# Score weights spread from one line by four products on one row group, and fewer, wider warm-up products, in a top-k cross-attention kernel

## The chip, the cores and the metric

The kernel runs on one core of a Trainium2 chip. The metric is the device time of one execution in microseconds; the time before is the median of three runs.

## What is computed

The reference, cut to what matters (B = 8 batches, N = 224 rows of x, S = 750 context rows, D = 512, 16 heads of 32, TOPK = 10):

```python
scores = jnp.einsum('bnd,d->bn', base_hidden, score_w[0]) + score_b[0]
_, topk_idx = jax.lax.top_k(scores, TOPK)
sparse_hidden = jnp.take_along_axis(base_hidden, topk_idx[:, :, None], axis=1)
q = (sparse_hidden @ Wq.T + bq)   # split into heads; k and v from scaffold_hidden (the context)
logits = jnp.einsum('bhqd,bhkd->bhqk', q, k) * scale
attn = jax.nn.softmax(logits, axis=-1)
o = jnp.einsum('bhqk,bhkd->bhqd', attn, v)
attn_out = o @ out_w.T + out_b
return base_hidden.at[jnp.arange(B)[:, None], topk_idx].set(attn_out)
```

All of it is float32.

## The kernel before

Each engine has its own hand-written program, and semaphores order them. The batches are taken in two groups: batches 0 and 1 first, then 2 to 7, so that attention on the first two can start while the other rows are still being scored.

The start runs as follows. SyncE's queue issues, in this order, x of batches 0 and 1, wq, x of 2, wk, x of 3 and 4, the context columns of batch 0 in two halves, x of 5 to 7, the columns of batch 1, and the context rows of 0 and 1. ScalarE's queue issues the score row (L265, into `score_quarters`, four partitions 0, 32, 64, 96, each with a quarter of the weights and the bias) and the biases (L266).

TensorE's program (L762 on) is: two warm-up products (`keep_warm(WARM_WEIGHTS)`, L561), `spread_score_w` (L567), which copies the score weights to 112 partitions by multiplying each quarter with a column of ones, ten warm-up products, `transpose_scores(0)` (L575), ten warm-up products, `spread_idx` (L581), `pick_rows` (L590, takes the chosen rows out of x by one-hot products), one warm-up product, `join_rows` (L600), `project_queries(0)` (L632), `fold_keys` (L645, folds the queries into the key weights, so keys are never formed), `dot_key_bias(0)` (L677), and the logits of batch 0 in the order in which the folded queries come (L700). A warm-up product multiplies a matrix of ones by 128 columns into a part of PSUM that nobody reads. TensorE executes its queue in order, so what stands behind a warm-up product waits for it.

VectorE copies the spread weights from PSUM (`copy_score_w`, L341, and the bias, L342) after one wait for all four products, forms the scores of a batch by two multiply-and-add passes over 112 partitions (L350), adds the bias (L363), and after the transposes finds the top ten with their positions (L366 to L376) and writes `idx_diag` (L378), for which L581 waits. After it come one-hot masks (L386), and ScalarE and VectorE copy the picked parts (L270, L393).

From then on TensorE alternates between logits (L700, L714) and mixing the context rows with the softmax weights (L731), with loads of context columns and rows issued as buffers come free; VectorE computes the shift of the softmax (L444 to L482) and ScalarE the exponential (L306). At the end the values are projected (L746), then the output (L758), and the rows are scattered into the output (L259).

Every float32 product at these lines stands in the trace as two weight loads (PEld) and two products (PE), each of one pass over the columns.

Of the kernel before, what the change touches and what calls it, by code (L numbers as in the profile page):

```python
# [21 lines left out]
B, N, D, S = 8, 224, 512, 750  # L22
HEADS, TOPK = 16, 10
DH = D // HEADS
P = 128
DT = D // P
# [4 lines left out]
X_P = N // 2  # L31
# [8 lines left out]
QUAD = 32  # L40
CB = HQ // QUAD
QUADS = P // QUAD
QK_UNITS = 2 * QK_STEPS
WARM_WEIGHTS, WARM_SCORES, WARM_CHOICE, WARM_N = 2, 10, 10, 128
FIRST = GROUPS[0][1]
PART = 32
TILE = 64
# [3 lines left out]
def build(nc, x, x_lines, ctx_rows, ctx_cols, wq, wk, wv, wo, in_bias, out_b, score_row, out):  # L51
# [5 lines left out]
    with stack:  # L57
        def sb(name, shape, dt=F32):
            return stack.enter_context(nc.sbuf_tensor(name, shape, dt))

        def ps(name, shape):
            return stack.enter_context(nc.psum_tensor(name, shape, F32))

        def sem(name):
            return stack.enter_context(nc.semaphore(name))
# [7 lines left out]
        bias_sb = sb("bias_sb", [P, 3, DT])  # L73
        out_b_sb = sb("out_b_sb", [BQ, D])
        score_w_sb = sb("score_w_sb", [X_P, D])
        score_quarters = sb("score_quarters", [P, P + 1])
        score_b_sb = sb("score_b_sb", [X_P, 1])
        ctx_c = [sb(f"ctx_c{n}", [P, DT, S_T, S_P]) for n in range(2)]
        ctx_r = [sb(f"ctx_r{n}", [P, S_T, D]) for n in range(2)]
# [1 line left out]
        ones = sb("ones", [P, P])  # L81
# [42 lines left out]
        logits_ps = [ps(f"logits_ps{n}", [P, 2, 512]) for n in range(2)]  # L124
# [6 lines left out]
        score_w_ps = mix_ps + misc_ps  # L131
# [9 lines left out]
        score_w_in, bias_in, out_b_in = sem("score_w_in"), sem("bias_in"), sem("out_b_in")  # L141
# [6 lines left out]
        score_w_ps_done, score_w_done = sem("score_w_ps_done"), sem("score_w_done")  # L148
# [113 lines left out]

        @block.scalar
        def _(act):
            act.dma_start(score_quarters[0:P:QUAD, :], score_row).then_inc(score_w_in, 16)  # L265
            act.dma_start(bias_sb[:, :, :], in_bias).then_inc(bias_in, 16)  # L266

            def copy_parts():
                act.wait_ge(parts_ps_done, 1)
                nc.scalar.activation(parts[:, 0:D // 2], parts_ps[0], ACT.Copy).then_inc(parts_done, 1)  # L270

            def copy_queries(g):
                b0, b1 = GROUPS[g]
                act.wait_ge(picked_T_ps, g + 1)
                nc.scalar.activation(picked_T[g][:, :, :], picked_ps[g][:, 0:DT * b1 * TOPK]  # L275
                                     .rearrange("p (t q) -> p t q", t=DT), ACT.Copy).then_inc(picked_T_done, 1)

            def copy_pairs():
                b0, b1 = GROUPS[1]
                for step in range(QK_STEPS):  # L280
                    act.wait_ge(pair_done, step + 1)
                    nc.scalar.activation(
                        qk[:, b0:b1, step, :].rearrange("p b (e r c) -> p r e b c", e=DT, r=2)[:, 0],
                        pair_ps[step % 2][0][:, 0:HQ // 2 * (b1 - b0)].rearrange("p (e b c) -> p e b c", e=DT, b=b1 - b0),
                        ACT.Copy).then_inc(low_copied, 1)

            def copy_fold():
                for step in range(QK_STEPS):
                    act.wait_ge(qk_ps, step + 1)
                    nc.scalar.activation(qk[:, 0:FIRST, step, :].rearrange("p b (e c) -> p e b c", e=DT),  # L290
                                         fold_ps[step][:, 0:HQ * FIRST].rearrange("p (e b c) -> p e b c", e=DT, b=FIRST),
                                         ACT.Copy).then_inc(qk_done, 1)

            def copy_key_rows():
                act.wait_ge(key_dot_ps, 1)
                for e in range(DT):
                    nc.scalar.activation(
                        key_rows[:, 0:FIRST, e, :],
                        key_ps[0][e * QUAD:(e + 1) * QUAD, 0:HC * FIRST].rearrange("p (b c) -> p b c", b=FIRST),
                        ACT.Copy).then_inc(key_rows_done, 1)  # L300

            def exponential(b, n):
                for k in range(2):
                    act.wait_ge(shifted, 2 * b + k + 1)
                    part = probs[n][:, k * BANK_T:(k + 1) * BANK_T, :]
                    nc.scalar.activation(part, part, ACT.Exp, scale=SCALE).then_inc(exp_done, 1)  # L306

            def copy_mix(b, half):
                act.wait_ge(mix_ready[half], b + 1)
                nc.scalar.activation(mix[:, 2 * half:2 * half + 2, :, b * TOPK:(b + 1) * TOPK],  # L310
                                     mix_ps[half][:, 0:2 * HQ].rearrange("p (t h q) -> p t h q", t=2, h=HEADS),
                                     ACT.Copy).then_inc(mix_out[half], 1)

            copy_parts()
            copy_queries(0)
            copy_fold()
            copy_key_rows()
            act.dma_start(out_b_sb[:, :], out_b.broadcast_to([BQ, D])).then_inc(out_b_in, 16)
            exponential(0, 0)
            copy_mix(0, 0)  # L320
            exponential(1, 1)
            copy_mix(0, 1)
            copy_mix(1, 0)
            copy_queries(1)
            copy_mix(1, 1)
            copy_pairs()
            exponential(2, 0)
            for b in range(3, B):
                copy_mix(b - 1, 0)
                exponential(b, b % 2)  # L330
                copy_mix(b - 1, 1)
            copy_mix(B - 1, 0)
            copy_mix(B - 1, 1)
# [2 lines left out]
        @block.vector  # L336
        def _(dve):
            def copy_score_w():
                dve.wait_ge(score_w_ps_done, 1)
                for r in range(QUADS):  # L340
                    nc.vector.tensor_copy(score_w_sb[:, r * P:(r + 1) * P], score_w_ps[r][0:X_P, 0:P]).then_inc(score_w_done, 1)  # L341
                nc.vector.tensor_copy(score_b_sb[:, :], score_w_ps[0][0:X_P, P:P + 1]).then_inc(score_w_done, 1)  # L342
                dve.wait_ge(score_w_done, QUADS + 1)

            def score(b, rows=(0, 1)):
                dve.wait_ge(x_in[b], 16)
# [164 lines left out]
            nc.vector.tensor_copy(row_name[:, :, :], row_name_i[:, :, :]).then_inc(vec_consts, 1)  # L511
            dve.wait_ge(vec_consts, 4)
            copy_score_w()
            score(0)
            score(1)
# [40 lines left out]

        @block.tensor
        def _(pe):
            def keep_warm(n):
                for _ in range(n):  # L560
                    nc.tensor.matmul(logits_ps[1][:, 1, 0:WARM_N], ones[:, :], ones[:, 0:1].broadcast_to([P, WARM_N]),  # L561
                                     start=True, stop=True)

            def spread_score_w():
                pe.wait_ge(score_w_in, 16)
                for r in range(QUADS):
                    last = nc.tensor.matmul(score_w_ps[r][0:X_P, 0:P + 1], ones[r * QUAD:r * QUAD + 1, 0:X_P],  # L567
                                            score_quarters[r * QUAD:r * QUAD + 1, :], start=True, stop=True)
                last.then_inc(score_w_ps_done, 1)

            def transpose_scores(g):
                b0, b1 = GROUPS[g]
# [11 lines left out]
            def pick_rows():  # L584
                pe.wait_ge(hot_done, 1)
                for half in range(2):
                    for b in range(FIRST):
                        for j in range(2):
                            at = (2 * b + j) * PART
                            last = nc.tensor.matmul(parts_ps[half][at:at + PART, :], one_hot[:, b, j, :],  # L590
                                                    x_sb[0:X_P, b, j, half * (D // 2):(half + 1) * (D // 2)],
                                                    start=True, stop=True)
                    last.then_inc(parts_ps_done, 1)

            def join_rows():
                pe.wait_ge(regroup_done, 2 * FIRST + 1)
                pe.wait_ge(parts_done, 2)
                for t in range(DT):
                    for j in range(P // TILE):
                        last = nc.tensor.matmul(picked_ps[0][j * TILE:(j + 1) * TILE, t * FIRST * TOPK:(t + 1) * FIRST * TOPK],  # L600
                                                parts[:, t * P + j * TILE:t * P + (j + 1) * TILE],
                                                regroup[:, :, :].rearrange("p b q -> p (b q)"), start=True, stop=True)
                last.then_inc(picked_T_ps, 1)
# [157 lines left out]

            pe.wait_ge(vec_consts, 1)  # L762
            keep_warm(WARM_WEIGHTS)
            spread_score_w()
            keep_warm(WARM_SCORES)
# [2 lines left out]
            keep_warm(WARM_CHOICE)  # L768
            spread_idx()
            pick_rows()  # L770
            keep_warm(1)
            join_rows()
            pe.wait_ge(wq_in, 16)
            project_queries(0)
# [58 lines left out]
```

## Time and profile before

| | |
|---|---|
| median of 3 runs | 148.5 us (148.49, 148.50, 149.54) |
| the profiled execution | 149.29 us, span 147.1 us |
| instructions in the span | 3011 |
| TensorE products (PE) | 136.9 us busy, 93%, 1292 records |
| TensorE weight loads (PEld) | 130.6 us busy, 89%, 1292 records |
| VectorE | 81.2 us busy, 55% |
| ScalarE | 23.2 us busy, 16% |
| GpSimd | 4.8 us busy, 3% |
| HBM traffic | 254 GB/s over the span |

The span is the time from the first to the last instruction of the profiled execution; 2.2 us of its time lie around it. Times in all rows are microseconds from the start of the span unless marked ns. PE stands for TensorE's products, PEld for its weight loads, DVE for VectorE, ACT for ScalarE, POOL for GpSimd, SP for SyncE; L and a number is the line of the kernel.

### The profile page before, as it was taken

Reading aid. Unit: us, or ns where it says so; the run is one execution under the profiler, and the core shown is the slowest. Engines: PE = TensorE matmul, PEld = TensorE weight load, DVE = VectorE, ACT = ScalarE, POOL = GpSimd, SP = SyncE. Lnnn points to the kernel's source line nnn. Section 1 sums busy time; section 2 is a strip of 40 time slices with the busy share of each in tenths; the row PEclk is TensorE's granted clock in tenths of the full one; section 3 lists DMA queues with packets and bytes.
Section 4 is the critical chain, followed back from the end, with each engine's and each line's share of the span. In section 5 each row is a group of like instructions: output and inputs, shape, how many; then the busy total and the mean of one; then the engine's idle time right before and its main releaser. Section 6 shows DMA issues by size and latency. Waiting matters only on the chain.

```text
span 147.1 us, 3011 instructions
## 1 busy us (share of the span) xinstructions
PE 136.9 (93%) x1292; PEld 130.6 (89%) x1292; DVE 81.2 (55%) x214; ACT 23.2 (16%) x48; POOL 4.8 (3%) x24
## 2 busy tenths in 40 slices
PE   3899868999999999999999999999999999999980
PEld 2896858999999998999999999999999999998840
DVE  1666654897893347457974286057318705745330
ACT  3001032002042034003041014004101400411100
POOL 6000000002000000000000000000000000000002
PEclk9999999999999999999999999999999999999999
DMA  4999999999857439989998994998691181000001
GB/s 150 417 423 414 417 416 426 370 419 415 250 226 254 178 77 391 399 317 417 413 408 274 301 347 125 304 300 331 196 324 46 20 357 50 0 4 0 4 0 45
DMA packets 5733, 37.61 MB, mean 256 GB/s; under 512 B 805, under 2 KB 809, under 8 KB 3417
## 3 DMA queue, kind: packets, MB, share of 16 engines
q1 hardware_dynamic: 5344, 36.93, 66.6%
q0 software_dynamic: 128, 0.33, 0.7%
q8 instruction: 10, 0.16, 0.5%
q10 hardware_dynamic: 248, 0.17, 0.4%
q14 instruction: 3, 0.02, 0.0%
HBM read 33.60 MB, written 3.83 MB: 254 GB/s over the span
## 4 chain that ended last, share of the span: by engine, by line
PE 89%; DVE 3%; issue 2%; DMA 2%; ACT 1%; POOLq 1%; DVEq 0%
PE mix_ps L731 36%; PE logits_ps L714 22%; PE logits_ps L700 11%; PE logits_ps L561 5%; PE logits_ps L632 3%; PE logits_ps L758 2%; DMA score_quarters<-score_row_dram 2%; PE logits_ps L666 1%; PE mix_ps L666 1%; PE misc_ps L746 1%; PE mix_ps L645 1%; ACT probs L306 1%; POOLq L57 1%; PE logits_ps L590 1%; PE misc_ps L645 1%
## 5 line engine op out<-in xcount | busy, mean ns | idle before, releaser
L731 PE MATMUL mix_ps<-probs,ctx_r 125*128 125x160 f32 x384 | 54.0, 300 | 0.2 <-ACT probs L306 0.2
L731 PEld LDWEIGHTS mix_ps<-probs,ctx_r 125*128 125x128 f32 x384 | 52.6, 190 | 1.0 <-issue 0.9
L714 PE MATMUL logits_ps<-qk,ctx_c 128*125 128x160 f32 x240 | 33.4, 300 | 0.0
L714 PEld LDWEIGHTS logits_ps<-qk,ctx_c 128*125 128x125 f32 x240 | 32.9, 188 | 0.0
L444 DVE TENSOR_REDUCE col_max<-logits_ps 125x160 f32<-125x960 f32 x8 | 9.2, 1154 | 25.7 <-PE logits_ps L714 21.3
L700 PE MATMUL logits_ps<-qk,ctx_c 128*125 128x160 f32 x144 | 20.5, 302 | 0.0
L700 PEld LDWEIGHTS logits_ps<-qk,ctx_c 128*125 128x125 f32 x144 | 19.6, 188 | 0.5 <-issue 0.4
L310 ACT ACTIVATE mix<-mix_ps 128x320 f32<-128x320 f32 x16 | 7.0, 439 | 64.5 <-PE mix_ps L731 64.5
L482 DVE TENSOR_REDUCE prob_sum<-probs 125x160 f32<-125x960 f32 x8 | 14.6, 1837 | 4.0 <-ACT probs L306 4.0
L306 ACT ACTIVATE probs<-probs 125x480 f32<-125x480 f32 x16 | 9.3, 603 | 28.1 <-DVE probs L476 28.1
L561 PE MATMUL logits_ps<-ones 128*128 128x128 f32 x46 | 9.3, 378 | 1.1 <-DVE ones L507 1.1
L350 DVE CUSTOM_DVE_ANT_0 product<-x_sb,score_w_sb 112x512 f32<-112x512 f32 x16 | 10.1, 681 | 0.0
L561 PEld LDWEIGHTS logits_ps<-ones 128*128 128x128 f32 x46 | 8.6, 284 | 1.8 <-DVE ones L507 1.1
L476 DVE TENSOR_TENSOR probs<-logits_ps,shift 125x480 f32<-125x480 f32 x16 | 9.8, 653 | 0.3
L632 PE MATMUL logits_ps<-picked_T,wq_sb 128*64 128x20 f32 (+1 forms) x128 | 4.1, 218 | 0.4 <-ACT picked_T L275 0.4
L632 PEld LDWEIGHTS logits_ps<-picked_T,wq_sb 128*64 128x64 f32 x128 | 3.9, 138 | 0.7 <-issue 0.7
L259 POOL DMA_INDIRECT out_dram<-y_sb,row_idx x1 | 0.9, 922 | 110.1 <-DVE y_sb L504 110.1
L466 DVE COPY head_shift<-head_shift 32x5 f32<-32x5 f32 x24 | 3.9, 163 | 0.8
L405 DVE TENSOR_TENSOR q_sb<-logits_ps,bias_sb 128x40 f32<-128x40 f32 (+1 forms) x4 | 1.0, 242 | 6.1 <-PE logits_ps L632 6.1
L454 DVE COPY quad_max<-quad_max 32x5 f32<-32x5 f32 x24 | 3.8, 160 | 0.8
L487 DVE RECIPROCAL inv_sum<-misc_ps 128x320 f32<-128x320 f32 x1 | 2.2, 2157 | 3.5 <-PE misc_ps L684 3.5
L758 PE MATMUL logits_ps<-wo_sb,o_T 128*80 128x256 f32 x16 | 3.7, 382 | 0.0
(97 smaller groups left out, 74.0 us busy)
## 6 DMA issues: line engine op xcount, KB each, us to landing
ctx_r<-ctx_rows_dram SPq DMA_DIRECT2D x8, 1536.0 KB, 7.7
ctx_c<-ctx_cols_dram SPq DMA_DIRECT2D x6, 1500.0 KB, 8.4
x_sb<-x_lines_dram SPq DMA_DIRECT2D x8, 512.0 KB, 10.6
out_dram<-x_sb SPq DMA_DIRECT2D x8, 448.0 KB, 12.6
ctx_c<-ctx_cols_dram SPq DMA_DIRECT2D x4, 750.0 KB, 15.8
wq_sb<-wq_dram SPq DMA_DIRECT2D x1, 1024.0 KB, 6.7
wk_sb<-wk_dram SPq DMA_DIRECT2D x1, 1024.0 KB, 9.7
wv_sb<-wv_dram SPq DMA_DIRECT2D x1, 1024.0 KB, 8.6
```

The costliest lines, as they stand in the source:

```text
L306: nc.scalar.activation(part, part, ACT.Exp, scale=SCALE).then_inc(exp_done, 1)
L310: nc.scalar.activation(mix[:, 2 * half:2 * half + 2, :, b * TOPK:(b + 1) * TOPK], mix_ps[half][:, 0:2 * HQ].rearrange("p (t h q) -> p t h ...
L350: nc.vector.tensor_tensor_reduce(out=products[j][:, :], in0=x_sb[0:X_P, b, j, :], in1=score_w_sb[:, :], scale=1.0, scalar=0.0, op0=ALU.mul ...
L444: nc.vector.tensor_reduce(col_max[0:S_P, :], tiles(n).rearrange("p k t c -> p c k t"), AX.XY, ALU.max)\
L476: nc.vector.tensor_tensor(probs[n][:, k * BANK_T:(k + 1) * BANK_T, :], tiles(n)[:, k, :, :], shift[0:S_P, :].unsqueeze(1).broadcast_to([S_ ...
L482: nc.vector.tensor_reduce(prob_sum[:, b, :], probs[n][:, :, :].rearrange("p t c -> p c t"), AX.X, ALU.add)\
L561: nc.tensor.matmul(logits_ps[1][:, 1, 0:WARM_N], ones[:, :], ones[:, 0:1].broadcast_to([P, WARM_N]), start=True, stop=True)
L632: last = nc.tensor.matmul(query_ps[g][half][j * TILE:(j + 1) * TILE, k * nq:(k + 1) * nq], wq_sb[:, t, c:c + TILE], picked_T[g][:, t, b0 * ...
L700: last = nc.tensor.matmul(logits_ps[n][0:S_P, t // BANK_T, (t % BANK_T) * HQ:(t % BANK_T + 1) * HQ], ctx_c[n][:, f, t, :], qk[:, b, f, :], ...
L714: last = nc.tensor.matmul(logits_ps[n][0:S_P, t // BANK_T, (t % BANK_T) * HQ:(t % BANK_T + 1) * HQ], ctx_c[n][:, f, t, :], qk[:, b, f, :], ...
L731: last = nc.tensor.matmul(mix_ps[half][:, f * HQ:(f + 1) * HQ], ctx_r[n][0:S_P, t, c:c + P], probs[n][:, t, :], start=(t == 0), stop=(t == ...
L758: last = nc.tensor.matmul(logits_ps[0][0:BQ, half, 0:D // 2], o_T[:, e, :], wo_sb[:, e, cols], start=(e == 0), stop=(e == DT - 1))
```

## The change

The score weights lie in one line of one partition (`score_line`, 512 weights and the bias). The four products that spread them all read partition 0, each signals its own end, and VectorE copies each as it comes; the bias is the last column of the fourth. The number of the products is still four (QUADS and DT are both 4). The warm-up products get widths of their own: one of 256 columns in place of two of 128 ahead of the weights, 512, 256 and 128 in place of ten of 128 ahead of the transposes, 512, 256 and 256 in place of ten of 128 ahead of the index spread, and one of 128 as before ahead of the join.

```diff
-WARM_WEIGHTS, WARM_SCORES, WARM_CHOICE, WARM_N = 2, 10, 10, 128
+WARM_WEIGHTS, WARM_SCORES, WARM_CHOICE, WARM_PARTS = (256,), (512, 256, 128), (512, 256, 256), (128,)
-        score_quarters = sb("score_quarters", [P, P + 1])
+        score_line = sb("score_line", [1, D + 1])
-            act.dma_start(score_quarters[0:P:QUAD, :], score_row).then_inc(score_w_in, 16)
+            act.dma_start(score_line[:, :], score_row).then_inc(score_w_in, 16)
             def copy_score_w():
-                dve.wait_ge(score_w_ps_done, 1)
-                for r in range(QUADS):
+                for r in range(DT):
+                    dve.wait_ge(score_w_ps_done, r + 1)
                     nc.vector.tensor_copy(score_w_sb[:, r * P:(r + 1) * P], score_w_ps[r][0:X_P, 0:P]).then_inc(score_w_done, 1)
-                nc.vector.tensor_copy(score_b_sb[:, :], score_w_ps[0][0:X_P, P:P + 1]).then_inc(score_w_done, 1)
-                dve.wait_ge(score_w_done, QUADS + 1)
+                nc.vector.tensor_copy(score_b_sb[:, :], score_w_ps[DT - 1][0:X_P, P:P + 1]).then_inc(score_w_done, 1)
+                dve.wait_ge(score_w_done, DT + 1)
-            def keep_warm(n):
-                for _ in range(n):
-                    nc.tensor.matmul(logits_ps[1][:, 1, 0:WARM_N], ones[:, :], ones[:, 0:1].broadcast_to([P, WARM_N]),
+            def keep_warm(widths):
+                for n in widths:
+                    nc.tensor.matmul(logits_ps[1][:, 1, 0:n], ones[:, :], ones[:, 0:1].broadcast_to([P, n]),
                                      start=True, stop=True)
             def spread_score_w():
                 pe.wait_ge(score_w_in, 16)
-                for r in range(QUADS):
-                    last = nc.tensor.matmul(score_w_ps[r][0:X_P, 0:P + 1], ones[r * QUAD:r * QUAD + 1, 0:X_P],
-                                            score_quarters[r * QUAD:r * QUAD + 1, :], start=True, stop=True)
-                last.then_inc(score_w_ps_done, 1)
+                for r in range(DT):
+                    c = P + (r == DT - 1)
+                    nc.tensor.matmul(score_w_ps[r][0:X_P, 0:c], ones[0:1, 0:X_P], score_line[:, r * P:r * P + c],
+                                     start=True, stop=True).then_inc(score_w_ps_done, 1)
-            keep_warm(1)
+            keep_warm(WARM_PARTS)
```

On the host, `score_row` becomes one row of 513 numbers in place of four of 129.

## Rows read from the trace of the kernel before

**Rows 1.** The page: busy us, share and instructions of each engine; the instruction queue.
```profile
PE 136.9 (93%) x1292; PEld 130.6 (89%) x1292; DVE 81.2 (55%) x214; ACT 23.2 (16%) x48; POOL 4.8 (3%) x24
...
q8 instruction: 10, 0.16, 0.5%
```

**Rows 2.** The chain in order of time, 16 to 28 us: start, us, what.
```profile
16.01 2.05 PE logits_ps L632 x64
...
20.63 1.91 issue
...
22.88 5.63 PE logits_ps L700 x40
```

**Rows 3.** The timeline, 4 to 13 us: start, us, engine and line, idle before.
```profile
4.13 0.56 PE L567 MATMUL mix_ps<-score_quarters,ones 1*112 1x129 f32 x2 [1.84 <-DMA score_quarters<-score_row_dram]
4.14 0.56 PE L567 MATMUL misc_ps<-score_quarters,ones 1*112 1x129 f32 x2
...
4.48 0.42 PE L567 MATMUL mix_ps<-score_quarters,ones 1*112 1x129 f32 x2
...
5.06 0.49 DVE L341 COPY score_w_sb<-mix_ps 112x128 f32<-112x128 f32 x2 [2.70 <-PE misc_ps L567]
...
5.86 0.15 DVE L342 COPY score_b_sb<-mix_ps 112x1 f32<-112x1 f32 x1
6.05 0.69 DVE L350 CUSTOM_DVE_ANT_0 product<-x_sb,score_w_sb 112x512 f32<-112x512 f32 x1
...
8.62 0.23 DVE L363 TENSOR_SCALAR biased_scores<-scores,score_b_sb 112x4 f32<-112x4 f32 x1
...
9.28 0.58 PE L575 MATMUL misc_ps<-ident,biased_scores 112*2 112x112 f32 x2
...
12.07 0.23 DVE L378 SCALAR_TENSOR_TENSOR idx_diag<-top_idx,row_base,own_batch 2x20 f32<-2x20 uint32 x1
...
12.58 0.37 PE L581 MATMUL misc_ps<-idx_diag,ones 2*112 2x20 f32 x2
```

**Rows 4.** Timeline of TensorE from 5.5 and from 11.1; L561's durations in both.
```profile
5.22 4.05 PE L561 MATMUL logits_ps<-ones 128*128 128x128 f32 x18
...
10.93 1.73 PE L561 MATMUL logits_ps<-ones 128*128 128x128 f32 x14
...
L561 PE MATMUL logits_ps<-ones 128*128 128x128 f32 x17 | 4.0, 431 | 0.0
...
L561 PE MATMUL logits_ps<-ones 128*128 128x128 f32 x12 | 1.5, 273 | 0.0
```

**Rows 5.** Who waited for whom, TensorE's products: us in total, times, longest.
```profile
PE logits_ps L677 <- issue: 1.9, 1, 1.9
...
PE mix_ps L731 <- ACT probs L306: 0.2, 1, 0.2
```

**Rows 6.** DMA queue of instructions in windows 20:21, 26.6:28, 40.6:42: packets, MB, share.
```profile
q8 instruction: 1, 0.02, 6.9%
...
q8 instruction: 1, 0.02, 4.9%
...
q8 instruction: 1, 0.02, 4.0%
```

**Rows 7.** Windows: length, TensorE busy (records), clock, DMA share, GB/s.
```profile
0.00:16.00 16.00, 12.18 (x90) 1.00 0.90 358
...
0.00:20.70 20.70, 16.80 (x221) 1.00 0.93 369
...
0.00:40.70 40.70, 34.77 (x354) 1.00 0.95 375
...
136.81:139.16 2.35, 2.35 (x129) 1.00 0.04 7
```

**Rows 8.** DMA issues in 5.4:6.95 and 6.95:9.7 us: count, KB each, median us to landing.
```profile
x_sb<-x_lines_dram SPq DMA_DIRECT2D x3, 512.0 KB, 15.2
...
ctx_c<-ctx_cols_dram SPq DMA_DIRECT2D x2, 750.0 KB, 18.7
```

More of the change, by code:

```diff
@@ L820 @@
         "out_b": np.asarray(L0_xattn_out_b).reshape(1, D),
-        "score_row": np.concatenate([np.asarray(L0_xattn_score_w).reshape(QUADS, P),
-                                     np.tile(np.asarray(L0_xattn_score_b).reshape(1, 1), (QUADS, 1))], axis=1),
+        "score_row": np.concatenate([np.asarray(L0_xattn_score_w).reshape(1, D),
+                                     np.asarray(L0_xattn_score_b).reshape(1, 1)], axis=1),
     }
```

## The prediction

> **What bounds the kernel.** I read the page first: TensorE's products are busy 93% of the span [rows 1], so time is won where TensorE is held up or does what nobody needs. The chain of work that ended last, in order of time, tells where that is. Up to 23 us it runs over the landing of the score row, warm-up products (L561), two small products for the choice of rows (L575, L581), the query and key products, and 1.91 us called "issue" [rows 2]. From 22.9 us on it is logits and mixing products back to back. All that the change touches lies before 16 us. A microsecond won there is won at the end, if nothing later absorbs it: the longest wait of TensorE's products after the 1.9 us one is 0.2 us [rows 5], and the transfers, which could absorb it, are looked at below.
>
> The timeline of 4 to 13 us [rows 3] shows who holds whom. L567's eight records run in two rounds of four, 4.13 to 4.92, since the four products lie on four different row groups. VectorE copies from 5.06 and scores from 6.05. The sum with the bias (L363) ends at 8.85, but L575 starts at 9.28, because ten warm-up products stand before it in TensorE's queue. idx_diag (L378) ends at 12.30, but L581 starts at 12.58, again behind ten. So in this execution warm-up holds the path by 0.39 and 0.25 us.
>
> The clock of TensorE doubles inside the second ten. The granted-clock column says 1.00 throughout, but the spacing tells it [rows 4]: 18 records from 5.22 span 4.05 us, which is (4.05 - 0.43) / 17 = 0.213 us from start to start; 14 from 10.93 span 1.73 us, (1.73 - 0.27) / 13 = 0.112. That is 1.66 and 0.875 ns per column, the levels 1.2 and 2.4 GHz at two cycles a column. Until then TensorE had been working without a gap since 4.13.
>
> **Part 1, the score weights.** One row of 2 KB in one partition is sent in place of four of 0.5 KB; the transfer is mostly latency (L567 waits for it until 4.13, rows 3), and I take its landing as unchanged, within 0.3 us either way. The four products now use the same row group, so eight records follow each other. From rows 3 and 4: the second starts 0.35 after the first (4.13, 4.48), the rest 0.213 apart, the last at 4.13 + 0.35 + 6 x 0.213 = 5.76, and it ends 0.42 later, 6.18. The copies run behind the products, which hides three of them: the fourth starts 0.14 after its product (as 5.06 after 4.92), 6.32. Then come one copy's spacing, 0.20 (four in 5.06 to 5.86), and the bias copy's, 0.19. The first score starts at 6.71 instead of 6.05: **+0.66 us**. The three added waits are covered by the products. The bounds: +0.5 if the products pack a little closer, +0.95 with the late landing. Rows 3 show what is given up: products on different row groups start 0.01 us apart (4.13, 4.14). The Trainium skill, "TensorE: Matmul & The Clock Gate", Part 3 (row/col tiling), speaks against this part: small products whose operands start at partitions 0, 32, 64 and 96 run at once, those on one row group do not; by its figure of 3.07 times for four packed products the eight records would take about 2.4 us instead of 0.79, an estimate, and the score would start at 7.0; by the rows it is 6.71.
>
> **Part 2, the warm-up products.** L575's data is now ready at 8.85 + 0.66 = 9.51. The warm-up ahead of it is 512 + 256 + 128 = 896 columns, two records each: 2 x 896 x 1.66 ns = 2.98 us. It starts at about 6.1 with 0.16 for its first gap (4.85 to 5.22), and ends its issue near 9.25. It no longer holds L575, which starts at 9.54, 0.26 later than before instead of 0.66 later. idx_diag then ends at 12.30 + 0.26 = 12.56. The second warm-up is 1024 columns, 2048 with both records. If the clock doubles at 10.93 as before, 1.02 us from 9.91 do 613 of them and the other 1435 take 1.26 us: done at 12.19, under VectorE's chain. L581 starts at 12.60 instead of 12.58. So of the 0.66 us, 0.02 to 0.1 is left in this execution; I take **+0.05**. keep_warm between picking and joining is one product of 128 columns as before.
>
> In an execution whose clock doubles before 8.5 us the old kernel loses nothing to warm-up: 0.39 + 0.25, and L575's second record follows 0.1 sooner and is shorter, together about 0.8 us (estimate from rows 3 and 4). The profiled execution took 149.29 us (span 147.1 and 2.2 around it), and the three runs 148.49, 148.50 and 149.54. The difference of 0.8 to the two fast ones is just that size. I take them for such executions; there the whole **+0.66** is paid.
>
> **Part 3, the instruction stream.** Each product at this line is two weight loads and two products. Fifteen fewer calls (23 before, 8 after) are 60 instructions less. This matters for the 1.91 us. L677 waits for nothing between its eight records, yet three run and five come 1.91 us later [rows 2, 5]. In that gap the only odd transfer is one packet of the instruction queue between 20 and 21 us [rows 6]. The page has ten such packets for 2 x 1292 TensorE instructions, 258 for each (rows 1 and 6), so one per 129 records. The stall comes at record 221. Counting back 129, TensorE passed record 92 at 16.07 us (90 by 16.0, rows 7). A packet near 40.7 us comes at record 354 [rows 6, 7], 133 after the stall, and TensorE waits for nothing there. So passing one block boundary asks for the block after the next boundary. From 16.07 to the restart at 22.55 is 6.5 us; the next boundary is passed at 22.55 and its packet comes after 26.6 [rows 6], again four microseconds in the crowd of loads. The block between took only 4.6 us to execute, because L632 runs a record each 0.032 us [rows 2] and L645 is of the same kind. That is why just this one is late.
>
> With 30 records fewer ahead, the first boundary falls at old record 122, 16.01 + 32 x 0.032 = 17.03, and the block is there at 23.5. The second falls at old record 251: with the stall gone L700 starts at 20.97, and 25 of its records later, at 5.63 / 40 = 0.141 each, it is 24.5. Cover 1.0 us; **the stall goes, -1.91**.
>
> **What would absorb it.** Everything from L700 on starts 1.9 us earlier. The context columns of batch 1 are issued from 6.99 and land 18.7 later in the median, near 26 [rows 8], where the second logits, now at 27.8, take them in halves; those of batch 0 stand ahead of the last x loads in the queue and land before them. The last three x loads are issued from 5.46 and take 15.2 in the median [rows 8], so they land from about 20 to 23; VectorE, held by the same stall today, would want them at 22.5, 23.7 and 25.0 (two records of 0.69 each, rows 3, at 0.61 spacing). All later loads are issued on TensorE's progress and move with it. Nothing takes the 1.9 back.
>
> **Sum.** Profiled execution: 149.29 - 1.91 + 0.05 = 147.4. Against the median: 148.5 - 1.91 + 0.66 = 147.25. The runs shown are what will be compared, so I forecast **147.2 us**, and 146.6 if the median execution is one where the 0.66 is covered.
>
> **Rivals.**
> - *The wait for code moves and does not vanish* (15%). The stall falls into L700 if the block takes over a microsecond longer than 6.5. For it: one sample, in a full DMA queue. Against it: cover 1.0 us. At its full price: 148.5 + 0.66 = 149.2; half of it, 148.2.
> - *The idle is not code* (5%). If the first 442 instructions and the next lie in TensorE's memory from the start, the 1.91 us has another cause, tied to the key products themselves, and stays: 148.5 + 0.66 = 149.2. The packet at 20 us, and ten packets in all, speak against it. The Trainium skill, "Runtime: NRT & Kernel Launch", Instruction fetch mechanics, is on this rival's side: it gives TensorE room for 2048 instructions and calls the refills mostly hidden.
> - *The clock stays at 1.2 GHz* (10%), the slower one. TensorE now idles from 9.25 to 9.54 and does 1.7 us of one-row products at 4.13, where it had worked on without a gap before its clock rose. It decides at 12.6: if the clock is low there, the second warm-up ends at 9.91 + 2048 x 1.66 ns = 13.3, L581 waits 0.7, L590 (16 records of 256 columns, four at a time) costs 4 x 256 x 0.79 ns = 0.8 more, and L632's 2.05 us [rows 2] up to 2.05 more, of which I take 1.8: 147.25 + 3.3 = 150.6.
> - *A wait for code at the end* (5%). A boundary falls late in L746 (129 records in 2.35 us, rows 7) and its block is asked for some 4 us earlier. The queues are idle then; up to 1 us: 148.2.
> - Mine: 65%, 146.6 to 147.9.
>
> **Range and chances.** 146.3 (row landing early, warm-up cover) to 149.4 (stall stays). A measurement of this kernel tells about 1% from no change, so faster means below 147.0. My case is split by that line: faster 0.33, within 1% 0.56 (with the rivals at 148 to 149.6), slower 0.11.
>
> **What would show it.** Right: L567 one after another, first score near 6.7, L575 waiting for L363, no issue wait at L677, L700 starting near 21 instead of 22.8 and L731 as much earlier, and the later steps unchanged. Wrong: an issue wait inside L700 or L746; L561 still 0.21 us per 128 columns after 11 us and L590 or L632 longer; or a landing of score_line well after 4.1.

## The result

The changed kernel takes 146.4 us (median of 4 runs, 146.26 to 146.50) against 148.61 for the kernel before (4 runs, 148.49 to 149.54). The ratio is 0.984, 95% interval 0.980 to 0.987: faster by 1.6%. Forecast were 147.2 us and 0.9%, with more chance for "within 1%" than for "faster"; the time lies inside the range, near its lower end, and the gain is nearly twice the one forecast. Two later sets of six runs gave ratios of 0.989 (0.982 to 0.995) and 0.988 (0.983 to 0.993). All sixteen executions of the changed kernel have a median of 146.44 us, with thirteen from 145.97 to 147.32 and three from 148.1 to 149.0. The second set alone has a median of 147.04. Executions of one kernel differ by up to some microseconds here, so medians are given with their extremes. The profiled execution took 146.49 us, its span 144.3, 2.8 less than before.

The timeline of the profiled changed kernel (start, us, engine and line, what it writes and reads, idle before):

```profile
0.74 0.51 ACTq L265 DMA_DIRECT2D score_line<-score_row_dram  x1
...
2.22 1.19 PE L568 MATMUL mix_ps<-score_line,ones 1*112 1x128 f32 x4
...
3.21 1.06 PE L568 MATMUL misc_ps<-score_line,ones 1*112 1x128 f32 x4
...
4.51 0.15 DVE L342 COPY score_b_sb<-misc_ps 112x1 f32<-112x1 f32 x1
4.69 0.69 DVE L350 CUSTOM_DVE_ANT_0 product<-x_sb,score_w_sb 112x512 f32<-112x512 f32 x1
...
7.29 0.23 DVE L363 TENSOR_SCALAR biased_scores<-scores,score_b_sb 112x4 f32<-112x4 f32 x1
...
7.67 0.53 PE L575 MATMUL misc_ps<-ident,biased_scores 112*2 112x112 f32 x2
...
10.69 0.37 PE L581 MATMUL misc_ps<-idx_diag,ones 2*112 2x20 f32 x2 [0.18 <-DVE idx_diag L378]
...
18.42 0.35 PE L677 MATMUL logits_ps<-q_diag,key_rep 128*32 128x80 f32 x8
18.69 5.70 PE L700 MATMUL logits_ps<-qk,ctx_c 128*125 128x160 f32 x40
```

Three things are to be seen beside [rows 2, 3]. The products that spread the weights start at 2.22 us instead of 4.13. They run one after another and the first score starts 2.47 us behind them instead of 1.92. And L677 runs all its eight records without a pause, so that L700 starts at 18.69. The queues show what became early. In the kernel before, whose timeline this is, the same load took twice as long to issue, beside the first two x loads:

```profile
0.75 0.85 SPq L186 DMA_DIRECT2D x_sb<-x_lines_dram  x2
0.75 1.09 ACTq L265 DMA_DIRECT2D score_quarters<-score_row_dram  x1
```

The DMA queues' packets say where the time went: those of ScalarE's queue (q10) beside those of SyncE's (q1), first from 1.6 to 1.8 us in the changed kernel, then from 3.3 to 4.1 us in the kernel before, which has none of q10 between 1.6 and 3.3 (packets, MB, share of 16 engines; half of the q10 packets shown carry the row, the other half its signals):

```profile
q1 hardware_dynamic: 5, 0.02, 35.3%
q10 hardware_dynamic: 2, 0.00, 3.4%
```

```profile
q10 hardware_dynamic: 8, 0.00, 1.2%
```

In both kernels the first packets of x start at 1.77 us. The packet of the row starts at 1.65 in the changed kernel, ahead of them, and takes 0.1 us. In the kernel before, where the issue ended at 1.84, the four packets start at 3.53 and take 0.03 us each: the row was waiting, not moving.

By L700 the changed kernel is 4.1 us ahead. It arrives with 2.8. This is where the rest went, in the timeline of the changed kernel, 23.9 to 26.5 us:

```profile
24.00 0.69 DVE L350 CUSTOM_DVE_ANT_0 product<-x_sb,score_w_sb 112x512 f32<-112x512 f32 x1 [0.51 <-DMA x_sb<-x_lines_dram]
...
25.35 0.23 DVE L363 TENSOR_SCALAR biased_scores<-scores,score_b_sb 112x12 f32<-112x12 f32 x1
...
25.64 0.35 PE L575 MATMUL misc_ps<-ident,biased_scores 112*6 112x112 f32 x2 [1.24 <-DVE biased_scores L363]
```

The last x load lands at 24.0 us (at 23.1 in the kernel before, where VectorE came to it at 26.8). VectorE waits for it, scores it, and TensorE, which has put the transposes of the second group into the middle of the logits of batch 0, waits 1.24 us for VectorE (1.55 and 0.56 us in the other two profiles of this kernel, where it landed at 24.3 and 23.5). The chain of the changed kernel now runs over that transfer, which none of the edits makes earlier:

```profile
6.39 17.59 DMA x_sb<-x_lines_dram
```

A table of the two profiled executions, start of each step in us:

| step | before | after | ahead |
|---|---|---|---|
| spread of the weights | 4.13 | 2.22 | 1.91 |
| first score (L350) | 6.05 | 4.69 | 1.36 |
| L581 | 12.58 | 10.69 | 1.89 |
| L632 | 16.01 | 14.13 | 1.88 |
| L700 of batch 0 | 22.81 | 18.69 | 4.12 |
| L731 of batch 0 | 37.14 | 34.35 | 2.79 |
| end of span | 147.1 | 144.3 | 2.8 |

### The profile page after: what moved, and what is told of

Its sections match the earlier page's. It is cut to its first block, busy times and chain, and to the rows that moved or that the text cites. A ratio compares the mean times of both kernels' runs of the same rounds, so it can differ in the third digit from the quotient of the medians.

```text
span 144.3 us, 2951 instructions
## 1 busy us (share of the span) xinstructions
PE 136.3 (94%) x1262; PEld 127.3 (88%) x1262; DVE 81.8 (57%) x214; ACT 23.1 (16%) x48; POOL 4.7 (3%) x24
## 4 chain that ended last, share of the span: by engine, by line
PE 76%; DMA 12%; SPq 4%; DVE 3%; issue 1%; POOLq 1%; ACT 1%; DVEq 0%
PE mix_ps L731 37%; PE logits_ps L714 23%; DMA x_sb<-x_lines_dram 12%; PE logits_ps L700 7%; PE logits_ps L758 3%; SPq L186 2%; PE logits_ps L666 2%; PE logits_ps L632 1%; PE mix_ps L666 1%; DVE product L350 1%; PE misc_ps L746 1%; ACT probs L306 1%; POOLq L57 1%; PE logits_ps L746 1%; SPq L179 1%
## 5 line engine op out<-in xcount | busy, mean ns | idle before, releaser
L731 PE MATMUL mix_ps<-probs,ctx_r 125*128 125x160 f32 x384 | 54.0, 300 | 0.2 <-ACT probs L306 0.2
L731 PEld LDWEIGHTS mix_ps<-probs,ctx_r 125*128 125x128 f32 x384 | 52.5, 190 | 1.0 <-issue 0.9
L700 PE MATMUL logits_ps<-qk,ctx_c 128*125 128x160 f32 x144 | 20.5, 301 | 0.0
L700 PEld LDWEIGHTS logits_ps<-qk,ctx_c 128*125 128x125 f32 x144 | 19.6, 188 | 0.5 <-issue 0.4
L482 DVE TENSOR_REDUCE prob_sum<-probs 125x160 f32<-125x960 f32 x8 | 14.6, 1836 | 4.0 <-ACT probs L306 4.0
L350 DVE CUSTOM_DVE_ANT_0 product<-x_sb,score_w_sb 112x512 f32<-112x512 f32 x16 | 10.4, 688 | 1.1 <-DMA x_sb<-x_lines_dram 1.1
L561 PE MATMUL logits_ps<-ones 128*128 128x256 f32 (+2 forms) x16 | 7.6, 615 | 1.1 <-DVE ones L507 1.1
L561 PEld LDWEIGHTS logits_ps<-ones 128*128 128x128 f32 x16 | 4.1, 284 | 3.8 <-issue 2.5
L632 PE MATMUL logits_ps<-picked_T,wq_sb 128*64 128x20 f32 (+1 forms) x128 | 4.1, 218 | 0.4 <-ACT picked_T L275 0.4
L632 PEld LDWEIGHTS logits_ps<-picked_T,wq_sb 128*64 128x64 f32 x128 | 3.9, 138 | 0.7 <-issue 0.7
## 6 DMA issues: line engine op xcount, KB each, us to landing
x_sb<-x_lines_dram SPq DMA_DIRECT2D x8, 512.0 KB, 10.9
```

What stands on the lines that cost most here:

```text
L350: nc.vector.tensor_tensor_reduce(out=products[j][:, :], in0=x_sb[0:X_P, b, j, :], in1=score_w_sb[:, :], scale=1.0, scalar=0.0, op0=ALU.mul ...
L482: nc.vector.tensor_reduce(prob_sum[:, b, :], probs[n][:, :, :].rearrange("p t c -> p c t"), AX.X, ALU.add)\
L561: nc.tensor.matmul(logits_ps[1][:, 1, 0:n], ones[:, :], ones[:, 0:1].broadcast_to([P, n]), start=True, stop=True)
L632: last = nc.tensor.matmul(query_ps[g][half][j * TILE:(j + 1) * TILE, k * nq:(k + 1) * nq], wq_sb[:, t, c:c + TILE], picked_T[g][:, t, b0 * ...
L700: last = nc.tensor.matmul(logits_ps[n][0:S_P, t // BANK_T, (t % BANK_T) * HQ:(t % BANK_T + 1) * HQ], ctx_c[n][:, f, t, :], qk[:, b, f, :], ...
L731: last = nc.tensor.matmul(mix_ps[half][:, f * HQ:(f + 1) * HQ], ctx_r[n][0:S_P, t, c:c + P], probs[n][:, t, :], start=(t == 0), stop=(t == ...
```

## The experiments

TensorE's granted clock differs between executions here: in four profiles (`e1_line`, `e2_warm`, `e4_bias_first`, `e9_wide`) it falls to half in a stretch that lies between 14.6 and 23.3 us. The mean granted clock of the whole execution, which stands on record for every execution, is 0.969 to 0.977 in those four. It does not show a late first rise: before the rise that column reads 1.00 as well, as in the kernel before, whose L561 ran at 1.66 ns a column until 10.9 us.

**The early row: two ways to make it late again.** In `e4_bias_first` ScalarE's two loads change places; in `e5_four_pieces` the row goes into the one partition in four pieces of 516 bytes (the products' reads and the row on the host follow, not shown).

```diff
 e4_bias_first, against the changed kernel
-            act.dma_start(score_line[:, :], score_row).then_inc(score_w_in, 16)
             act.dma_start(bias_sb[:, :, :], in_bias).then_inc(bias_in, 16)
+            act.dma_start(score_line[:, :], score_row).then_inc(score_w_in, 16)
```

```diff
 e5_four_pieces, against the changed kernel
-        score_line = sb("score_line", [1, D + 1])
+        score_line = sb("score_line", [1, QUADS, P + 1])
-            act.dma_start(score_line[:, :], score_row).then_inc(score_w_in, 16)
+            act.dma_start(score_line[:, :, :], score_row[:, :, 0:P + 1]).then_inc(score_w_in, 16)
```

> The changed kernel with ScalarE's two loads exchanged: the biases (128 partitions) are issued first, the score line second, so that the line is issued behind the first x loads. Theory A (the row came early since its one packet was put in ahead of the x packets): L568 starts at 3.5 to 4.5 instead of 2.2; of that delay about 1.2 us is covered by the wait for the last x load; median 147.0 to 147.6. Rival D (it came early since it is one packet in one partition, wherever it stands): L568 starts before 3.2; median under 146.7.

> The changed kernel with the score row sent into one partition in four pieces of 516 bytes (gaps between them in DRAM) instead of one of 2052. Theory A1 (the four pieces are what made the issue of the load take 1.09 us and put it behind the x packets): the issue takes about 1.1 us again and L568 starts near 4.1; fastest executions 147.2 to 147.8. Theory A2 (four partitions, spread over several DMA engines, are what did it): issue 0.5 us, L568 at 2.2 to 2.5, fastest executions near 146.4.

Timeline of `e4_bias_first`, then of `e5_four_pieces`:

```profile
1.18 0.54 ACTq L266 DMA_DIRECT2D score_line<-score_row_dram  x1
...
4.71 0.55 PE L568 MATMUL mix_ps<-score_line,ones 1*112 1x128 f32 x1 [2.42 <-DMA score_line<-score_row_dram]
```

```profile
0.76 1.19 ACTq L265 DMA_DIRECT2D score_line<-score_row_dram  x1
...
4.10 1.19 PE L568 MATMUL mix_ps<-score_line,ones 1*112 1x128 f32 x4 [1.81 <-DMA score_line<-score_row_dram]
```

The line issued in 0.54 us, but 0.4 us later, is used 2.5 us later: 148.0 us (147.74 to 150.63, 11 executions, ratio 0.996, interval 0.993 to 0.999). The line in four pieces takes 1.19 us to issue and is used when the quarters were: 147.23 us (146.99 to 148.58, 10 executions, ratio 0.992, interval 0.989 to 0.996). The packets fit both. In `e5` those of the row start at 3.36 to 3.49, behind the first of x (1.75); in `e4` the one packet starts at 3.96, behind those of x and behind all 128 packets of the biases in its own queue. So the row is early where its one piece is issued before the first x packets go (1.75 to 1.77 in all these runs); that it lies in one partition is not enough. Whether `e4` is late for its 0.4 us or for standing behind the biases is not separated. Rival D is out. `e4` came out above its range (147.0 to 147.6): L568 started at 4.71, later than the 3.5 to 4.5 that I had put. In `e5` Theory A1 holds, with its fastest executions at 146.99, a little under the range. `e5` is the changed kernel with the landing that the prediction assumed, and it takes what the prediction said: 147.2. Part of that agreement is luck, since the terms are off one by one, as shown below.

**The wait at L677: the count of instructions alone.** `e3_count` cuts the same columns into more products, `e9_wide` merges those of the kernel before.

```diff
 e3_count, against the changed kernel (60 instructions more)
-WARM_WEIGHTS, WARM_SCORES, WARM_CHOICE, WARM_PARTS = (256,), (512, 256, 128), (512, 256, 256), (128,)
+WARM_WEIGHTS, WARM_SCORES, WARM_CHOICE, WARM_PARTS = (128,) * 2, (128,) * 7, (64,) * 11 + (160,) * 2, (128,)
```

```diff
 e9_wide, against the kernel before (60 instructions fewer)
-WARM_WEIGHTS, WARM_SCORES, WARM_CHOICE, WARM_N = 2, 10, 10, 128
+WARM_WEIGHTS, WARM_SCORES, WARM_CHOICE, WARM_PARTS = (256,), (512, 512, 256), (512, 512, 256), (128,)
```

> The changed kernel with the same warm-up columns (256, 896, 1024, 128) cut into 2, 7, 13 and 1 products instead of 1, 3, 3 and 1: 60 instructions more, nothing else. Theory A: the issue wait is back inside L677, 1.3 to 2 us; up to 1.2 us of it is covered by the wait for the last x load, which falls in L575's wait; median 0.3 to 0.8 above the changed kernel's 146.4. Rival B: no issue wait, the same time within 0.2.

> The kernel before with its warm-up columns unchanged (256, 1280, 1280, 128) but in 1, 3, 3 and 1 products instead of 2, 10, 10 and 1; quarters and four row groups as before. Only the count of TensorE's instructions falls, by 60. Theory A: no issue wait at L677, L575 and L581 start as before (9.3 and 12.6 or earlier), the clock behaves as in the kernel before; fastest executions 146.0 to 146.6, median 146.6 to 147.2. Rival B (the wait belongs to the key products): the wait stays, median 148.2 to 148.6.

TensorE's timeline in `e3_count` near L677:

```profile
18.97 0.33 PE L677 MATMUL logits_ps<-q_diag,key_rep 128*32 128x80 f32 x3
20.67 0.34 PE L677 MATMUL logits_ps<-q_diag,key_rep 128*32 128x80 f32 x5 [1.38 <-issue]
```

The wait is back, after the same third record of eight, although L677 runs 1.3 us earlier than in the kernel before. Of all that the change took out, only the 60 instructions were put back; the row is as early and the columns are as few as in the changed kernel. It is 1.38 us here, inside what was expected. The time is not: 148.72 us (147.41 to 152.15, 10 executions, ratio 0.998, interval 0.993 to 1.003) against an expected 146.7 to 147.2. Two things besides the wait are in it. A pass of 64 columns takes 0.112 us at the higher clock, as much as one of 128, so the second warm-up takes 3.3 us instead of 2.5 and L581 starts 0.55 later in the profile (147.41 us). And three of the ten executions are above 150; two of these have a mean granted clock of 1.000, and none was profiled, so their cause is open. `e1_line` below has the same count with 1280 columns in each warm-up and has none above 149.6.

`e9_wide` says what the count is worth: 146.96 us (146.29 to 149.44, 7 executions) against 148.16, ratio 0.990, interval 0.987 to 0.993. Its profile has no wait at L677. It is one of those with the low clock, though, where L632 and L645 take longer and would by themselves give the code its time; the verdict rests on the times of its other executions. A clean profile without the 60 instructions and without the early row is that of `e2_again`, next. The gain in the medians, 1.2 us, is less than the wait seen in the one profile of the kernel before (1.9 to 2.2 us); why is open.

**The warm-up edit without the line.** `e2_warm` and `e2_again` are one kernel: the warm-up of the changed kernel, 1024 + 896 columns instead of 2560, and the quarters.

```diff
 e2_warm, against the kernel before
-WARM_WEIGHTS, WARM_SCORES, WARM_CHOICE, WARM_N = 2, 10, 10, 128
+WARM_WEIGHTS, WARM_SCORES, WARM_CHOICE, WARM_PARTS = (256,), (512, 256, 128), (512, 256, 256), (128,)
```

> Score weights in four quarters on four row groups as before, only the warm-up products as in the changed kernel. Theory A: L567 starts at 4.1 and the four quarters are spread by 4.9, the first score starts near 6.05; no issue wait at L677, L700 starts 2.2 to 2.6 us earlier than in the kernel before; the last x load is no bound; median 146.3 to 146.9. Rival B: the issue wait stays, median 148.2 to 148.6. Rival C (the clock of TensorE doubles later with fewer warm-up columns): L561 still at 1.66 ns a column after 11 us, median above 149.

> The kernel with quarters and the fewer, narrower warm-up in total (256, 896, 1024, 128 columns), once more. Theory G (with 384 + 256 columns less after an unchanged start, TensorE pauses before L575 and its clock often rises late or falls again before L632, so the fewer columns cost what the fewer instructions gain): executions spread from 146.3 to 152, the larger part above 148, and slower than the same with 1280 and 1280 columns. Theory A: mostly 146.3 to 147.2.

Ten executions: 147.20 and 147.41, then eight from 149.44 to 152.12; median 151.15, and in the second set a ratio of 1.012 (1.006 to 1.017), slower than the kernel before. The two profiles show both cases. TensorE in windows of `e2_again` (147.41 us) with its timeline at L677, then in windows of `e2_warm` (150.52 us): length, busy time and records, granted clock, DMA share, GB/s:

```profile
15.50:22.00 6.50, 6.08 (x156) 1.00 1.02 416
```

```profile
20.51 0.35 PE L677 MATMUL logits_ps<-q_diag,key_rep 128*32 128x80 f32 x8
20.78 5.70 PE L700 MATMUL logits_ps<-qk,ctx_c 128*125 128x160 f32 x40
```

```profile
15.50:22.00 6.50, 6.08 (x112) 0.56 1.02 416
```

In the first nearly the whole second warm-up runs at 1.2 GHz (3.47 us for its 1024 columns) and the clock rises at its end; there is no wait at L677 and L700 starts at 20.78, 2.03 ahead of the kernel before, with the full clock and the row as late (L567 at 4.19). In the second the clock rose as late, at about 12.8, and was granted at half again from 16.2: 112 records in the time of 156. With 1280 and 1280 columns (`e9_wide`) one execution of seven was above 149; with 896 and 1024 behind the same late row, eight of ten. Theory G holds. Both signs of Rival C came true as well: L561 still ran at 1.66 ns a column after 11 us, and the median is above 149. `e2_again`'s profile rose as late and took 147.41 us, so in `e2_warm`'s it was the fall after it that cost the time. The five slowest (151.8 to 152.1) have a mean granted clock of 1.000, so no fall like that; a rise later still would fit them, but none was profiled.

**The line without the warm-up edit.** `e1_line` has the line, the early row and the old 2, 10, 10 and 1 products of 128 columns.

> The line and its four products on one row group as in the changed kernel, the warm-up products as before (2, 10, 10 and 1 of 128 columns), so 60 TensorE instructions more than the changed kernel. Theory A (row lands 1.9 us early; the 1.91 us wait is for instructions; what is over after both is taken back by the last x load near 24 us): L568 starts at 2.2; warm-up holds L575 until about 8.6 instead of 7.7; an issue wait of 1.5 to 2 us is back inside L677; median 147.0 to 147.6. Rival B (the wait has nothing to do with the count of instructions, and went with the earlier start): no issue wait at L677; median 146.4 to 146.8.

It takes 147.87 us (147.24 to 149.60, 10 executions, ratio 0.995, interval 0.992 to 0.998), a little over the expected range. L568 starts at 2.22 as expected. L575 starts at 8.22, held by its ten products, 0.4 earlier than expected, since here the clock had risen before it (its two records span 0.35 us instead of 0.53). The issue wait was not seen: this profile, too, has the low clock (0.54 from 15.5 to 22), L632 takes 3.56 us instead of 2.05, and the block of code has its time. For the wait this run is inconclusive; for the whole it shows that the early row without the warm-up edit brings 0.5%.

**The changed kernel again.** `after_again` and `after_third` are the changed kernel itself.

> The changed kernel once more, in more executions. Theory A (the four executions seen happened to be without a fall of TensorE's clock between L590 and L645, which the profiles of the last three kernels with a longer time showed): most executions near 146.4, some between 148 and 150. Rival E (the changed kernel's warm-up keeps the clock up whatever the moment at which it first rises): all within 146.0 to 146.8.

> The changed kernel in one call with the tuned later choice, on the same chip. From ten executions so far (146.0 to 149.0): median 146.3 to 147.1, one in four above 147.

147.04 us (146.0 to 149.0) and 146.28 us (145.97 to 148.14), six executions each. Theory A holds, but rarely: three of sixteen are above 148. None of the three profiles fell on one of them, but the record has their mean granted clock: 0.987, 0.969 and 0.977, the three lowest of the sixteen, where the others have 0.992 or more. So a fall of the clock goes with them; where in the execution it fell is not shown.

**A later choice, to take the last x load off the path.** VectorE's order and two places in TensorE's change; the choice for batches 2 to 7 has some six microseconds to spare before L616 needs its rows (issued at 30.1, landed 7.7 later, first used at 44.2 in the changed kernel).

```diff
 e8_tuned, against the changed kernel (e7_later_choice has 22 and 6 for 20 and 8)
+            find_max(0, 0)
+            find_shift(0)
+            subtract_max(0, 0)
             choose_eight(1)
             choose_rest(1)
-            find_max(0, 0)
-            move_idx()
-            find_shift(0)
-            subtract_max(0, 0)
             find_max(1, 1)
+            move_idx()
             find_shift(1)
-            logits_by_step(0, 0, [qk_done], {20: lambda: transpose_scores(1)})
+            logits_by_step(0, 0, [qk_done], {})
             pe.wait_ge(key_rows_done, DT)
-            logits_by_step(1, 1, [], {8: move_idx})
-            weigh(0, 0, {})
+            logits_by_step(1, 1, [], {20: lambda: transpose_scores(1)})
+            weigh(0, 0, {8: move_idx})
```

> The changed kernel with the choice for batches 2 to 7 moved behind the softmax shift of batch 0: VectorE does L444 to L476 of batch 0 first and L363 to L378 of the second group after it; TensorE's L575 of that group moves from the logits of batch 0 into those of batch 1, and L608 into the mixing of batch 0. Theory A (the landing of the last x load near 24 us holds TensorE at L575 for 1.2 us and delays the first mixing): no wait at L575, first L731 near 32.4 instead of 34.35, some 0.5 us of it lost again before the second batch; fast executions 1.2 to 1.8 below the changed kernel's. Rival F (the gather of the rows becomes late, L616 waits): no gain or slower.

> The kernel with the later choice, L575 of the second group two tiles earlier in the logits of batch 1 and L608 two places later in the mixing of batch 0, against 0.97 us that VectorE waited or sat idle around L575 and 0.34 us that TensorE waited at L608. Theory A: no wait at L608, L616 0.5 us earlier relative to the first L731; median 145.6 to 146.1. Rival H (the gain is lost before the second batch's mixing, where the exponential comes late): 146.1 to 146.5.

> The tuned later choice again, beside the changed kernel. Theory A (the wait for the last x load no longer lies on TensorE's path): median 145.7 to 146.2, and 0.4 to 0.9 below the changed kernel's on the same chip. Rival H (its lower median came from another chip): within 0.3 of it.

TensorE's timeline of `e8_tuned` around that place:

```profile
19.51 12.28 PE L700 MATMUL logits_ps<-qk,ctx_c 128*125 128x160 f32 x88
31.63 0.36 PE L575 MATMUL misc_ps<-ident,biased_scores 112*6 112x112 f32 x2
...
32.92 2.34 PE L731 MATMUL mix_ps<-probs,ctx_r 125*128 125x160 f32 x16
35.19 0.44 PE L608 MATMUL misc_ps<-ones,idx_diag 2*80 2x1 f32 x4
```

Eighty-eight records without a pause where the changed kernel stopped at the fortieth, and L731 starts at 32.92 instead of 34.35, although the row landed 0.8 us later in this execution (L568 at 3.06). `e7` took 146.28 us (146.17 to 146.53, 6 executions), with 0.34 us of wait at L608. Its gain misses the expected 1.2 to 1.8: the changed kernel beside it had 147.04, and 146.0 in its fastest execution. `e8` took 145.90 (145.73 to 146.46) and, beside the changed kernel on one chip, 145.83 (145.72 to 146.07) against 146.28 (145.97 to 148.14). That is 0.3% below the changed kernel, five of its six below all six of the other, and 1.8% below the kernel before (0.982, interval 0.979 to 0.986). The intervals of the two ratios against the kernel before overlap (0.983 to 0.993 for the changed kernel). All eleven executions of `e8` lie below 146.5. The gathered rows now land at 43.1 us with L616 at 43.6, so this slack is used up. The profile of `e8_again` shows the next bound, 0.56 us of wait for the first half of the context columns of batch 1:

```profile
PE logits_ps L700 <- DMA ctx_c<-ctx_cols_dram: 0.6, 1, 0.6
```

## Why the prediction was off

- **The landing of the score row** (part 1, "I take its landing as unchanged, within 0.3 us either way"): this step failed. It came 1.91 us earlier. I had called the wait until 4.13 "mostly latency". It was place in a queue: the packets of the row started 1.7 us after their issue had ended and took 0.03 us each. The kernel before showed a sign of it: the issue of 2 KB took 1.09 us, while the two x loads of 512 KB each were issued beside it in 0.85. `e5_four_pieces`, which undoes this step alone, takes 147.23.
- **The spread on one row group** (+0.66): from L568's start to the first score 2.47 us, against 1.92 before, +0.55; the lower end of the bounds was 0.5. The products run at 0.21 us each as summed, and the last starts 1.63 behind the first as summed; the copies end closer behind them. The eight records took 2.05 us, as summed from the rows, and not the 2.4 us of the other estimate there.
- **The warm-up no longer holds L575 and L581** (+0.05 of the 0.66 left): with the earlier row taken out, L581 is 0.02 us late (1.89 ahead of 1.91). Right in the profiled pair. That the whole 0.66 is paid in executions with an early clock was the reason for 147.2 instead of 146.6; that it is paid whole then is borne out by the profiles of `e9_wide` (quarters) and `e5_four_pieces` (line), both with an early clock: their spreads start at 4.07 and 4.10, L581 at 11.78 and 12.36, which is 0.55 more behind the landing. That the runs of the kernel before at 148.5 have an early clock was not seen in a profile.
- **The wait for code** (-1.91): right in kind. It is gone, it follows the count of instructions to the record (`e3_count`), and the count alone is worth 1% (`e9_wide`). Its size in the profiled pair was a little more: L581 to L700 took 10.23 us before and takes 8.00, which is 2.23 less (9.70 in `e3_count`, 8.01 in `e5`). In the medians it is less, 1.2 us (`e9_wide`). The chain's 1.91 begins at the modelled end of the last record, 0.25 us after its start.
- **Nothing takes it back** (what would absorb it): right for a gain of 1.9, wrong for 4.1. The x loads were put at 20 to 23 us against a need at 25.0; with the row early as well, the need moved ahead of the last landing, 24.0, and 1.3 us went there. The last load also landed 0.9 later than the 23.1 of the kernel before. So the early row is worth some 0.8 us (medians 147.23 to 146.44) and not 1.9. The size is rough: beside `e5` on one chip the changed kernel had 147.04, and the ratios against the kernel before are 0.992 for `e5` and 0.984 to 0.989 for the changed kernel.
- **The sum, term by term, in the profiled pair**: forecast -1.91 + 0.05, 149.29 to 147.4. Measured -1.91 (landing) + 0.02 (what was left at L581) - 2.23 (wait for code) + 1.33 (lost up to L731), which is -2.79; 146.49 us. The landing put at nothing is by far the largest miss, and the loss at the last x load took back two thirds of it. That the time came out within 0.8 us of the forecast is owed to these two misses of opposite sign.
- **The chances**: the line at 1% ran through my own case. The missing 0.8 us decided it.
- **Rivals**: the wait that moves, the idle that is not code and the wait at the end did not come true. The clock rival, at 10% for this kernel, did not come true in its profiled executions, and three of its sixteen have a lowered clock, at 148.1 to 149.0 us. For the same warm-up behind a late row (`e2`) its size came true (151.2 against 150.6), but L590 ran at the higher clock and L632 at the lower. Left untested is the changed kernel with `e9_wide`'s 1280 and 1280 columns, so whether fewer columns help or harm behind the early row is open.

## What to carry to other kernels

Look at the first small load that a step waits for: here it paid to send it in one piece and to issue it ahead of the big loads, since its own packets took a tenth of a microsecond and its wait behind theirs nearly two. An idle time called issue inside a run of short products that wait for nothing can be code arriving late, as it was here; add or remove instructions ahead of it to see whether it follows, and merge those that do no work. When two gains sit in front of the same transfer, add them only as far as its landing.

## What the runs showed of the hardware

- A load of one row of 2052 bytes took 0.51 to 0.54 us to issue from ScalarE, in four pieces 1.09 (four partitions) or 1.19 (one partition). Where the issue ended at 1.25, the first product ran at 2.22; where it ended at 1.7 to 1.95, at 4.1 to 4.7. In the profiles of `e7_later_choice` and `e8_tuned` the packet of the row started as early as in the changed kernel (1.65), but took 1.1 us instead of 0.1, and the first product ran at 3.09 and 3.06; in `e8_again`, the same kernel, at 2.21. Why is open.
- TensorE's code comes in packets of some 258 instructions (ten for 2584), and the traces fit with the next block but one being asked for at each boundary. Behind the boundaries at its records 92 and 221 the packets started 4.0 and 4.2 us later in the kernel before and 3.6 and 3.8 in `e3_count`, but 2.7 and 2.2 in the changed kernel, counted in executed records; so the moment of the request is known only roughly. The Trainium skill, "Runtime: NRT & Kernel Launch", Instruction fetch mechanics, gives TensorE room for 2048 instructions; the wait after 442 of them, here and in `e3_count`, does not fit that, and the measurement decides.
- The granted clock can fall in a stretch where TensorE is mostly busy. In `e9_wide` it was 1.00 from 12 to 14.5 us and half after 15.5, at which the engine dropped from 2.4 to 1.2 GHz; in the changed kernel it stayed. TensorE's windows of `e9_wide`, then of the changed kernel:

```profile
12.00:14.50 2.50, 1.99 (x33) 1.00 1.04 429
15.50:22.00 6.50, 6.50 (x113) 0.50 1.02 416
```

```profile
12.00:14.50 2.50, 1.86 (x39) 1.00 1.04 429
15.50:22.00 6.50, 6.50 (x119) 1.00 1.02 414
```

TensorE was busy for 1.99 us of 2.5 where it fell and for 1.86 where it did not, so this measure does not tell which executions lose it. What does is open. The Trainium skill, "TensorE: Matmul & The Clock Gate", Part 1 (HAM oscillation), speaks of long waits between bursts as the cause. This trace has none: the pauses of TensorE's products in `e9_wide` between 11 us and the fall are 0.2 to 0.4 us each.
